# VectorE takes two neighbouring PSUM banks in one instruction

## The reference, cut to what matters

```python
xn = layernorm(x)
x = x + favor(xn) + local_ffn(xn)        # both branches read the same xn
xn = layernorm(x)
x = x + attention(xn) + mixture_of_experts(xn)

# favor: 16 heads, 32 random features a head, causal
score = exp(q features) . exp(k features)   # 256 x 256 a head and sequence
num, den = (score * causal) @ [v, 1]

# local_ffn, twice (two layers): 8 heads of 64, windows of 64
q, k = l2norm(q) * q_scale, l2norm(k) * k_scale
q = q * cos * scale + rotate_half(q) * sin * scale      # x8 for q
k = k * cos / scale + rotate_half(k) * sin / scale
o = softmax(q @ k^T inside a window and the one before it) @ v
x = x + o @ wo;  then a gated feed-forward
```

## Time and profile before

| | |
|---|---|
| median of 3 runs | 2262.85 us (2262.48 to 2275.0) |
| the profiled execution's own time | 2274.8 us |
| its span, first to last instruction | 2273.0 us |
| TensorE busy | 1854.6 us, 82% |
| VectorE busy | 1381.7 us, 61% |
| ScalarE busy | 766.9 us, 34% |
| mean granted TensorE clock | 0.929 of full |

### The profile page before, as it was taken

One profiled execution on the slowest core, in us unless ns is written; L12 is line 12 of the kernel. 1 busy time (PEld: TensorE's weight loads), 2 busy tenths in 40 slices (PEclk: granted clock), 3 DMA queues, 4 the chain that ended last, 5 costly groups with the idle time before them and its releaser, 6 DMA issues.

```text
span 2273.0 us, 43389 instructions
## 1 busy us (share of the span) xinstructions
PE 1854.6 (82%) x18044; PEld 1077.6 (47%) x18044; DVE 1381.7 (61%) x2973; ACT 766.9 (34%) x1401; POOL 293.7 (13%) x238
## 2 busy tenths in 40 slices
PE   1788898788887798877988779888797887988887
PEld 1445444454454553545535444455444554444544
DVE  1666557665566664766656655666556665576654
ACT  0332253223522236233252233422343323533234
POOL 0110101101111021011110111101101101011010
PEclk9998899998999999998999989998899988999889
DMA  4000200002000020000100020000200002000020
GB/s 171 1 1 2 33 2 6 1 2 33 7 2 1 2 33 7 2 1 14 22 6 2 2 29 7 6 1 3 33 2 6 1 2 33 3 6 1 2 28 7
DMA packets 27478, 29.79 MB, mean 13 GB/s; under 512 B 3524, under 2 KB 25844, under 8 KB 26740
## 3 DMA queue, kind: packets, MB, share of 16 engines
q1 hardware_dynamic: 27284, 27.01, 6.3%
HBM read 12.06 MB, written 2.36 MB: 6 GB/s over the span
## 4 chain that ended last, share of the span: by engine, by line
PE 51%; DVE 28%; ACT 6%; SPq 5%; DMA 5%; issue 5%; POOL 0%; ACTq 0%; DVEq 0%
PE bank L913 5%; SPq L414 4%; PE bank L697 4%; PE bank L903 3%; PE bank L729 3%; DMA phi<-parts 3%; PE bank L888 3%; DVE lc L1295 2%; DVE lrec L1365 2%; DVE lc L1347 2%; DVE ftm L1276 2%; PE bank L926 2%; PE bank L998 2%; PE bank L589 2%; DVE fp L1286 2%
## 5 line engine op out<-in xcount | busy, mean ns | idle before, releaser
L1522 DVE TENSOR_REDUCE amx<-bank 128x2 f32<-128x512 f32 x256 | 163.1, 686 | 76.1 <-PE bank L926 75.9
L1143 ACT ACTIVATE silu<-bank 128x512 f32<-128x512 f32 x144 | 84.2, 597 | 275.4 <-PE bank L888 263.3
L1511 DVE TENSOR_TENSOR mh<-bank,silu 128x512 f32<-128x512 f32 x144 | 98.8, 691 | 116.8 <-PE bank L903 108.5
L913 PEld LDWEIGHTS bank<-w_mw,mh 128*128 128x128 f32 x1152 | 151.0, 210 | 24.0 <-issue 24.0
L913 PE MATMUL bank<-w_mw,mh 128*128 128x128 f32 x1152 | 158.1, 297 | 0.0
L455 POOL TENSOR_TENSOR lc<-lc,ls 128x512 f32<-128x512 f32 x32 | 40.8, 1274 | 897.8 <-DVE lc L1295 895.8
L888 PE MATMUL bank<-xn2T,w_mw 128*128 128x512 f32 x288 | 145.6, 629 | 0.0
L1543 DVE RECIPROCAL ftm<-bank 128x512 f32<-128x512 f32 x16 | 53.7, 3358 | 145.2 <-PE bank L1005 145.2
L637 PE MATMUL bank<-hT,w_wqkv 128*128 128x512 f32 x256 | 119.0, 602 | 17.2 <-ACT hT L1034 11.0
L1295 DVE SCALAR_TENSOR_TENSOR lc<-bank,w_cols,w_rotary 128x512 f32<-128x512 f32 x128 | 93.4, 746 | 59.1 <-PE bank L637 59.1
L1353 DVE TENSOR_REDUCE lmx<-bank 128x4 f32<-128x512 f32 x128 | 79.6, 685 | 80.0 <-PE bank L697 80.0
(11 more groups left out here) (265 smaller groups left out, 3709.5 us busy)
## 6 DMA issues: line engine op xcount, KB each, us to landing
phi<-parts SPq DMA_DIRECT2D x96, 64.0 KB
lc<-parts SPq DMA_DIRECT2D x96, 64.0 KB
w_mw<-in_mw SPq DMA_DIRECT2D x3, 1152.0 KB
x_in<-in_x SPq DMA_DIRECT2D x8, 256.0 KB, 9.5
out<-res SPq DMA_DIRECT2D x8, 256.0 KB, 2.3
w_wqkv<-in_wqkv SPq DMA_DIRECT2D x1, 1536.0 KB
w_w<-in_w SPq DMA_DIRECT2D x1, 682.0 KB
w_rotary<-in_rotary SPq DMA_DIRECT2D x1, 512.0 KB
```

The lines of the kernel that those rows point to most:

```text
L913: last = mm(bank_of("final")[:, t], mh[:, (2 * q + i) % 4, t], W["mw2"][:, ORDER[q], i, :], start=(q == 0 and j == 0 and i == 0), stop=Fal ...
L1511: V.tensor_tensor(mh[:, n % 4, :], bank_of("moe_u", n)[:], silu[:, n % 2, :], ALU.mult).then_inc(sem["moe_h"], 1)
L1522: V.tensor_reduce(amx[:, 2 * b:2 * b + 2, h], bank_of("att_max", n)[:].rearrange("p (t k) -> p t k", t=2), AX.X, ALU.max).then_inc(sem["at ...
```

## The change

VectorE's instructions on two banks that lie side by side become one instruction over both. PSUM is declared as one tensor `banks` of eight banks so that an access can span two. Four places:

- Rotation: the four `scalar_tensor_tensor` of a pair become two `tensor_tensor` over both raw banks and 1024 columns. The head's scale columns are multiplied into the rotary tables once, ahead of the loop (`rot`, 16 more small instructions). A pair starts when both of its products are there, and one `loc_c` is raised after the second instruction, where before each half raised its own.
- Masks: two `tensor_tensor` of 768 columns for a quad instead of four of 384; `favor_p` counts pairs.
- Norm scaling: one `tensor_tensor` of 1024 columns for a pair instead of two of 512; `loc_qk` counts pairs.
- Maxima of the first group: two reductions over two banks instead of four. The second group keeps its four.

So that pairs lie side by side, `pair_of_banks` rounds the ring `short` up to an even place ahead of each quad and of each layer's raw products. Most jobs behind it land in another bank, whose last user is another. With the new rings, layer 0's `loc_max` products of the first group wait for: bank 0 and 1, `favor_p` 8 (quad 3, both pairs); bank 2, `loc_qk` 4 (scaling of pair 3); bank 3, `loc_qk` 3. Layer 1's, in the order in which they are issued: bank 2, `loc_qk` 8 (scaling of its pair 3); bank 3, `favor_p` 16; bank 0, `loc_qk` 6; bank 1, `loc_qk` 7. Quads 1 to 3 take banks 4, 5, 0, 1, the same four as the quad ahead of them.

```diff
-        bank = [ctx.enter_context(nc.psum_tensor(f"bank{i}", [P, 512], F32)) for i in range(8)]
+        banks = ctx.enter_context(nc.psum_tensor("bank", [P, 8, 512], F32))
+        bank = [banks[:, i, :] for i in range(8)]
...
+        rot = sb("rot", [P, DEPTH, 2, 4, SEQ])
...
-        cen = sb("cen", [P, T])
+        cx = sb("cx", [P, 2, T])
+        cen, xn2T = cx[:, 0, :], cx[:, 1, :]
...
-        lsb = [ls[:, 0, :], ls[:, 1, :], cen[:], xn2T[:]]
-        lrec = sb("lrec", [P, 2, SEQ])
+        lsb = [ls, cx]
+        lrec = ls[:, :, 0:SEQ]
...
+        fpt2 = [fp[:, i:i + 2, :] for i in (0, 2)] + [
+            more[:, 768 * i:768 * i + 768].rearrange("p (a k) -> p a k", a=2) for i in range(2)]
...
+        def pair_of_banks():
+            turns_of["short"] += turns_of["short"] % 2
+
         def favor_jobs(*slot):
             if slot in FAVOR_AT:
+                pair_of_banks()
                 quad = FAVOR_AT[slot]
                 if quad % 4 == 0:
                     job("favor_pv", quad // 4, "favor_att", quad // 4 + 1)
                 for n in range(4 * quad, 4 * quad + 4):
-                    job("favor_score", n, "favor_p", n + 1)
+                    job("favor_score", n, "favor_p", n // 2 + 1)
...
+            pair_of_banks()
...
-                job("loc_rb", 4 * l + p, "loc_qk", 8 * l + 2 * p + 2)
+                job("loc_rb", 4 * l + p, "loc_qk", 4 * l + p + 1)
...
+        def two_banks(name, k):
+            i = AT[name, k][0]
+            assert AT[name, k + 1][0] == i + 1, (name, k)
+            return banks[:, i:i + 2, :]
...
-                        pool.wait_ge(sem["loc_c"], now("loc_c", 2 * m + 2))
-                        nc.gpsimd.tensor_tensor(lc[:, c, :], lc[:, c, :], lsb[2 * (m % 2)],
+                        pool.wait_ge(sem["loc_c"], now("loc_c", m + 1))
+                        nc.gpsimd.tensor_tensor(lc[:, c, :], lc[:, c, :], lsb[m % 2][:, 1, :],
                                                 ALU.subtract).then_inc(sem["loc_rot"], 1)
-                        nc.gpsimd.tensor_tensor(lc[:, c + 1, :], lc[:, c + 1, :], lsb[2 * (m % 2) + 1],
+                        nc.gpsimd.tensor_tensor(lc[:, c + 1, :], lc[:, c + 1, :], lsb[m % 2][:, 0, :],
                                                 ALU.add).then_inc(sem["loc_rot"], 1)
...
-                    pe.wait_ge(sem["favor_p"], now("favor_p", 4 * quad + 4))
+                    pe.wait_ge(sem["favor_p"], now("favor_p", 2 * quad + 2))
...
-                        pe.wait_ge(sem["loc_qk"], now("loc_qk", 8 * l + 4 * g + 4))
+                        pe.wait_ge(sem["loc_qk"], now("loc_qk", 4 * l + 2 * g + 2))
...
-                        act.wait_ge(sem["loc_c"], now("loc_c", n + 1))
+                        act.wait_ge(sem["loc_c"], now("loc_c", n // 2 + 1))
...
+            for l in range(DEPTH):
+                for qk in range(2):
+                    for i, (trig, half) in enumerate(((0, 0), (0, 1), (1, 0), (1, 1))):
+                        ins = V.tensor_scalar(rot[:, l, qk, i, :], W["rotary"][:, 2 * qk + trig, :],
+                                              W["cols"][:, 2 + 4 * l + 2 * qk + half:3 + 4 * l + 2 * qk + half],
+                                              None, ALU.mult)
+                    made(ins)
...
-                        for n in range(4 * quad, 4 * quad + 4):
-                            dve.wait_ge(sem["favor_score_ps"], now("favor_score_ps", n + 1))
-                            V.tensor_tensor(fpt[n % 8], bank_of("favor_score", n)[:, 0:384], W["causal"][:],
+                        for n in (4 * quad, 4 * quad + 2):
+                            dve.wait_ge(sem["favor_score_ps"], now("favor_score_ps", n + 2))
+                            V.tensor_tensor(fpt2[n % 8 // 2], two_banks("favor_score", n)[:, :, 0:384],
+                                            W["causal"][:].unsqueeze(1).broadcast_to([P, 2, 384]),
                                             ALU.mult).then_inc(sem["favor_p"], 1)
 
                 for l in range(DEPTH):
                     for p, (qk, g) in enumerate(PAIRS):
                         m, c = 4 * l + p, 4 * qk + 2 * g
-
-                        def turned(out, half, trig):
-                            i = 2 + 4 * l + 2 * qk + half
-                            return V.scalar_tensor_tensor(out, raw[half], W["cols"][:, i:i + 1],
-                                                          W["rotary"][:, 2 * qk + trig, :].unsqueeze(1).broadcast_to([P, G, SEQ]),
-                                                          ALU.mult, ALU.mult)
-
-                        v3 = lambda a: a.rearrange("p (b t) -> p b t", b=G)
-                        raw = [v3(bank_of("loc_raw", 2 * m + ab)[:]) for ab in range(2)]
-                        part = [v3(lsb[2 * (m % 2) + ab]) for ab in range(2)]
-                        dve.wait_ge(sem["loc_raw_ps"], now("loc_raw_ps", 2 * m + 1))
+                        tabs = lambda i: rot[:, l, qk, i:i + 2, :].unsqueeze(2).broadcast_to([P, 2, G, SEQ])
+                        halves = lambda a: a.rearrange("p a (b t) -> p a b t", b=G)
+                        raw = halves(two_banks("loc_raw", 2 * m))
+                        dve.wait_ge(sem["loc_raw_ps"], now("loc_raw_ps", 2 * m + 2))
                         if p == 0:
                             if l:
                                 dve.wait_ge(sem["loc_sT_ps"], now("loc_sT_ps", 16))
                             else:
                                 dve.wait_ge(sem["att_pv"], prior("att_pv"))
-                        turned(v3(lc[:, c, :]), 0, 0)
+                        V.tensor_tensor(halves(lc[:, c:c + 2, :]), raw, tabs(0), ALU.mult)
                         if m >= 2:
                             dve.wait_ge(sem["loc_rot"], now("loc_rot", 2 * m - 2))
-                        turned(part[1], 0, 1).then_inc(sem["loc_c"], 1)
-                        dve.wait_ge(sem["loc_raw_ps"], now("loc_raw_ps", 2 * m + 2))
-                        turned(part[0], 1, 1)
-                        turned(v3(lc[:, c + 1, :]), 1, 0).then_inc(sem["loc_c"], 1)
+                        V.tensor_tensor(halves(lsb[m % 2][:]), raw, tabs(2), ALU.mult).then_inc(sem["loc_c"], 1)
...
-                        for c in (4 * qk + 2 * g, 4 * qk + 2 * g + 1):
-                            dve.wait_ge(sem["loc_rot"], now("loc_rot", 2 * m + c % 2 + 1))
-                            V.tensor_tensor(lc[:, c, :], lc[:, c, :], bank_of("loc_rb", m)[:], ALU.mult).then_inc(sem["loc_qk"], 1)
+                        c = 4 * qk + 2 * g
+                        dve.wait_ge(sem["loc_rot"], now("loc_rot", 2 * m + 2))
+                        V.tensor_tensor(lc[:, c:c + 2, :], lc[:, c:c + 2, :],
+                                        bank_of("loc_rb", m).unsqueeze(1).broadcast_to([P, 2, T]),
+                                        ALU.mult).then_inc(sem["loc_qk"], 1)
                         favor_heads(l, "rb", p)
                     for g in range(2):
-                        for i in range(4) if g == 0 else (3, 0, 1, 2):
+                        for i in (0, 2) if g == 0 else (3, 0, 1, 2):
                             h = 4 * g + i
+                            if g == 0:
+                                dve.wait_ge(sem["loc_max_ps"], now("loc_max_ps", 8 * l + h + 2))
+                                V.tensor_reduce(lmx[:, :, i:i + 2, 0].rearrange("p j i -> p i j"),
+                                                two_banks("loc_max", 8 * l + h).rearrange("p i (j k) -> p i j k", j=TT),
+                                                AX.X, ALU.max).then_inc(sem["loc_mx"], 2)
+                                continue
```

More of the change, by code:

```diff
@@ L147, in build @@
         for n, ap in w.items():
-            if n not in ("ones2", "block8", "projT"):
+            if n not in ("ones2", "rotary", "block8", "projT"):
                 W[n] = sb("w_" + n, list(ap.shape), ap.dtype)
@@ L495, in _ @@
             last.then_inc(prep_ps, 1)
-            pe.wait_ge(prep, 7)
+            pe.wait_ge(prep, 11)
             for g in range(2):
@@ L499, in _ @@
             last.then_inc(prep_ps, 1)
-            pe.wait_ge(prep, 10)
+            pe.wait_ge(prep, 14)
             pe.wait_ge(started, 9)
@@ L1199, in _ @@
             made(V.tensor_tensor(b1s[:, :], bank[0][:, 0:12], W["b1"][:], ALU.add))
-            assert done[0] == 8, done
+            assert done[0] == 12, done
             V.tensor_tensor(W["rows"][:, 3, :], W["rows"][:, 3, :], W["rows"][:, 6, :], ALU.add)
```

10 lines of the change are left out of this document (5 added, 5 removed).

## The result

The changed kernel takes 2355.43 us (median of 4 runs, 2351.25 to 2360.56) against 2265.3 us before in the same comparison (2262.48 to 2275.0): a ratio of 1.0378, 95% interval 1.0352 to 1.0404. It is 90 us slower, twice the 44.5 us that the prediction summed up and outside its range.

What follows compares the result with a forecast made beforehand. The prediction took the chain passing between TensorE and VectorE as the bound, so starts of the next engine count. Terms 1.1 + 2.0 + 1.55 + 0.9 = 5.55 us a turn, eight turns 44.5, gave 2262.85 + 44.5 = 2307 us, range 2268 to 2333.

Steps and rivals of the forecast that it cites:

- VectorE's price: Wide VectorE instructions take 1.22 us over 1024 columns, 0.95 over 768; a merge saves 0.065 us of step once.
- the waits for both products and both squares: Rotations, both layers: VectorE waits for a pair's second product, +0.86 us; squares wait for the second wide instruction, +0.11.
- the scores' wait for a whole quad: Layer 0 masks: quad 1's scores need all four masks of quad 0 instead of three, +0.34 us.
- the mask products' new bank: Layer 0, first maxima products: third bank now freed by the last scaling, ahead of all 96 products; stage +2.0 us a turn.
- +1.1 as summed: Layer 0 rotation: waits for squares and second product, 0.11 + 0.86 + 0.11 = 1.1 us a turn.
- the clock term of the sum: Layer 1: three more mask products behind the last scaling, 1.3 us at the half clock, 0.65 at the full one.
- The prediction's own last sign of being wrong: Whole kernel: the forecast would be wrong if the clock falls in other places than before.
- the maxima were put at nothing: First group's maxima end while TensorE is in the second group's products, cover 2.6 us, so counted as nothing.
- rival c: Faster, 2225 to 2240 us: VectorE's queue sets the end in all four places, saving 4.8 a turn; chance 0.06.
- (b): Delays swallowed, 2265 to 2285 us: scaling wait falls where TensorE is held anyway, last pairs' products come earlier; chance 0.14.
- (d): The wide access costs two full instructions or stalls, 2330 us and more; chance 0.03.
- Rival (a): Half clock spreads to layer 0's 96 products, 12 to 20 us more, 2320 to 2335 us in all; chance 0.25.

Runs made afterwards that it cites:

- 3: Changed kernel plus extra TensorE products in its waits (ahead of sums(0) or random-feature products, sums(1), first mask product): 1.0246 of before.
- 13: Changed kernel with rotation by narrow halves, a pair's first instruction waiting for both of its products: 1.0294 of before.
- 14: Changed kernel with rotation by narrow halves starting on the first product, both squares waiting for the pair's fourth instruction: 1.0182 of before.
- 4: Changed kernel with layer 1's sums(0) moved behind the fourth pair of raw products, all wide instructions kept: 1.0235 of before.
- 10: Changed kernel with rotation by halves and layer 0 quads from bank 0, masks narrow again: 0.9985 of before, against 0.9991 with wide masks.
- 11: Changed kernel with rotation by halves and layer 0 quads from bank 0, norm scaling narrow again: 0.9974 of before, against 0.9991 with wide scaling.
- 7: Kernel before with layer 1's sums(0) moved behind the fourth pair of raw products: 1.0055 of before.
- 16: Changed kernel with extra TensorE products only inside the rotations, none ahead of the mask products: 1.0272 of before.
- 9: Changed kernel with rotation by halves, layer 0 quads from bank 0, layer 1's sums(0) behind the fourth raw pair, and extra products: 1.0098 of before.

## Why the prediction was wrong in size

- **The direction and the waits held.** VectorE's price, the waits for both products and both squares, the scores' wait for a whole quad, the mask products' new bank: each is in the trace where it was put. With the fillers of 3 layer 1's rotation costs 12.6 us more than before (forecast 12.5). Layer 0's rotation goes from 23.6 to 24.7 us in the turns in which the clock is full, +1.1 as summed; the first turn, which the prediction's rows don't show, goes from 20.1 to 22.9 (3). Layer 0's norms, masks and scaling go from 14.9 to 16.8 in the first turn, where neither kernel works at 1.2 GHz in them: +1.9, forecast 2.0.
- **The step that failed is the clock term of the sum.** It was 1.3 us a turn, for three mask products of layer 1. The half clock of layer 0's 96 products was left to a rival of 12 to 20 us at a chance of 0.25, and layer 1's last raw products were put at the full clock without a reason. Both ran mostly at 1.2 GHz: 10.7 and 13.1 us, each shown by 3, in which both keep the full clock once the waits are filled. The prediction's own last sign of being wrong, the clock falling in other places than before, is the one that came. In other stages there was less work at 1.2 GHz than before. Over the whole trace there is 42 us more of it, which is at most 21 us of time, and the sum had about 5 of these; by the mean granted clock, 0.929 to 0.920, an estimate gives about 12 us (two executions of before on one chip took 2268.97 us at 0.935 and 2279.88 at 0.927).
- **A second step: the maxima were put at nothing.** The prediction let them end under the second group's products. In layer 1 the last mask product of that group waits for them, 0.46 us later than before in each turn, 3.7 us. No run tested the wide maxima by themselves.
- **What is left over.** The traces are 80 us apart, 35.5 more than the sum. The clock in net (at most some 16), the maxima (3.7) and the first turn of layer 0 (1.7) leave about 14 us that no run puts down to a cause.
- **The rotation.** Repairing it gave back 60 us by the medians and 49.5 by the traces, nearly all inside the two rotations, where the forecast's terms were 21. Of the two waits, the one for both products is worth 1.8 points and the late squares 0.7 (13, 14), each with the clock that came with it.
- **"VectorE sets the end" (rival c) fell** with 4: with all wide instructions kept, layer 1's rotation takes 15.3 us a turn once its products come early, against 15.8 before. "Swallowed" (b) fell with the idle times. "Dear in themselves" (d) fell with 1217 ns; its range, 2330 and more, took in the result, for another reason. Rival (a) named the right event in layer 0, but ended at 2335. What remained of use was small: wide masks and scaling are worth nothing measurable (10, 11).
- **The Trainium skill's advice** (VectorE: DVE Perf Modes, "Rules for kernel authors") to lower the count of instructions bought VectorE 34 us of busy time here. The section that the prediction cites also says that an instruction that isn't held starts earlier, and the steps of 0.60 us agree with that. What a merge costs or saves is set by the start of the neighbours: 0.065 us for a merged pair of masks or scalings by the steps in the trace, against 0.86 for a wait on the second product.
- **Baseline.** The costs were read in an execution of before of 2274.8 us and their sum was added to a median that is 12 us less. The 48 us between 2307 and 2355 are these 12 and the 35.5 above.
- **Open.** Why 7 is slower than before, why the repairs give back less together than alone, and what decides in which stage the clock falls: it differs from turn to turn of one trace, and executions of before on one chip spread over 11 to 15 us.

## What to carry to other kernels

Merging two instructions over two buffers saves a fixed part of a step once, and moves the start to the later input and the release to the later end; where the engine is idle ahead of that place, the merge costs the distance between the two inputs (0.86 us here), however fast it is. Rounding a ring of buffers to even places changes who frees every buffer behind it: write out the new releaser for each job and look for one that now comes later, since that alone cost 1.6% here. Count a wait of TensorE twice, once as itself and once as products that may run at 1.2 GHz behind it; filling it with extra products shows the second part, but here they paid only inside the rotations' waits (16); ahead of the mask products, where they ran past the end of the wait, they brought nothing, and where there was no wait they cost 1.9 us a turn (9).

## What the runs showed of the hardware

- One VectorE instruction over two PSUM banks, 1024 columns, takes 1211 to 1217 ns, the same as 1024 columns of SBUF (1219 before, 1211 after), and 768 columns take 950 ns. No cost of the second bank shows.
- A reduction over two banks with 8 results takes 1221 ns against 685 for one: two of them are 1370, so the wide one is 0.15 us shorter.
- With 9 and 7 extra products inside its waits, TensorE kept the full clock through both rotations (0 us of work at 1.2 GHz against 17 and 27 us), and the kernel with more work was 1.1 to 1.3% of before's time faster. The work at 1.2 GHz in the whole trace was 309 us without fillers and with all of them, and 294 with those of the rotations alone.
- In layer 1's rotation the wait ahead of sums(0) is 2.48 us long where it was 1.88, and the last two raw products behind it ran mostly at 1.2 GHz (3.27 us instead of 1.98, granted clock 0.62).
- The same kernel's time follows the granted clock: in seven executions of before on one chip, 2268.97 us at 0.935 up to 2279.88 us at 0.927.
